# Cross-attention and feed-forward: values computed and placed early, three written orders, one sum per tile

## The chip, the cores and the metric

The kernel runs on one core of a Trainium2 chip. The metric is the device time of the kernel in microseconds (us), the median of several executions; one more execution was recorded by the profiler, and all rows below come from that one.

## What is computed

`x` is 4 x 2048 rows of 512 numbers; each of the four batches has a context of 77 rows. 16 heads of 32.

```python
x = x + xattn(layernorm(x), ctx, mask, Wq, Wk, Wv, Wo)
#   q = xn @ Wq.T; k = ctx @ Wk.T; v = ctx @ Wv.T           (per head 32 wide)
#   probs = softmax(mask(q @ k.T / sqrt(32)))               (77 keys)
#   xattn = (probs @ v) @ Wo.T
x = x + ffn(layernorm(x), Win, bin_, W1, b1, W2, b2, Wout, bout)
#   s = xn @ Win + bin_                                      (64 units)
#   h = relu(s[..., None] * W1 + b1)                         (16 inner values each)
#   g = sum(h * W2, -1) + b2;  ffn = g @ Wout + bout
```

## The kernel before

**Groups and steps.** The 8192 rows are cut into 16 groups of 512 rows, each of 4 tiles of 128 rows. Matrix products run in float16 with a high and a low part of each operand, in three passes, so most values exist as two halves, "high" written by ScalarE (ACT) and "low" by VectorE (DVE) or GpSimd (POOL). The program is a software pipeline of steps i = -2 to 17. Step i works on five groups at once: AHEAD is the layer norm of group i+2, FRONT the queries of group i+1 (`q`, four 128-wide pieces), SOFT the softmax of group i, its `pv` and `wo` for tiles 0 and 1, BACK the rest of group i-1 (`pv` and `wo` of tiles 2 and 3, then `ffn_in` and the units `pre` 0 to 3), FFN the rest of group i-2 (`pre` 4 to 7, `g`, `out`, and the store). The softmax goes by eight halves k of a group (a tile has two halves of 8 heads x 77 keys, 616 columns): logits on PE (`lg`), `maxima` on DVE (row maximum, subtract), `exps` on ACT, `sums` on DVE for a tile (row sums, scaling, reciprocal), `divide` on POOL, `p_part` on ACT, `p_low` on POOL, and a transposing transfer `turn_p`. Steps -2 to 1 are written out, steps 2 to 13 are three laps of a hardware loop of four steps, and steps 14 to 17 are written out.

**Order.** Nothing is scheduled by a tool: each engine has one function `one_step` that lists its work in order, and runs it in that order, waiting on semaphores. One `one_step` serves all 20 steps; work whose group does not exist in a step is left out. PSUM is handed out by two rings of two banks each (`tr_banks`, `mm_banks`) in the order of the tables `TR_ORDER` and `MM_ORDER`.

**Transfers.** All transfers are issued by SyncE's queue (SP), in order, and a transfer that must wait holds everything behind it: `turn_p`, `turn_x`, `turn_h` (transposes of the probabilities and of the two normed inputs), `store`, `reload` of x (two halves a group), `next_keys`, and `next_values`. The latter fills `v_now`, two buffers of blocks of V as `pv` wants them: 12 transfers (`CUTS`) from `v_all` for one buffer, at every even step from 2 to 12; step 0 fills both buffers, 24 transfers. In the queue they stand behind `turn_p(3)` and ahead of `turn_x(0)`, `turn_h(2)` and `turn_h(3)`.

**Setup.** Before step -2, PE transposes the context, Wk and Wq and makes the keys. Wv and Wo (the part LATE: `late_values`, `late_wo`) come in step 0, between `wo(2)` and `pv(0, .)` in the lists: 16 transposes of Wv, 32 matmuls for V of four batches, 16 transposes of Wo. Small weights of the feed-forward part lie in the second buffer of `qT`, so the first piece of q of group 1 in step 0 (`q_part` on ACT) waits until `wout` has been placed by 16 transfers.

Of the kernel before, what the change touches and what calls it, by code (L numbers as in the profile page):

```python
# [67 lines left out]
ALL = (AHEAD, FRONT, SOFT, BACK, FFN)  # L68
FIRST_FULL = 2
# [5 lines left out]
TR_ORDER = (  # L75
    (FFN, "pre", 4), (FFN, "pre", 5), (FFN, "pre", 6), (FFN, "pre", 7), (FRONT, "q", 0), (FRONT, "q", 1),
    (FRONT, "q", 2), (FRONT, "q", 3), (LATE, "wvT", 0), (LATE, "wvT", 1), (LATE, "wvT", 2), (LATE, "wvT", 3),
    (LATE, "woT", 0), (LATE, "woT", 1), (LATE, "woT", 2), (LATE, "woT", 3), (BACK, "pre", 0), (BACK, "pre", 1),
    (BACK, "pre", 2), (BACK, "pre", 3),
)  # L80
MM_SETUP = [("k", c) for c in range(C)]
MM_ORDER = (
    (FFN, "g", 0), (FFN, "out", 0), (FFN, "out", 1), (FFN, "out", 2), (FFN, "out", 3), (BACK, "pv", 2),
    (BACK, "pv", 3), (BACK, "wo", 2), (LATE, "v", 0), (LATE, "v", 1), (LATE, "v", 2), (LATE, "v", 3), (BACK, "wo", 3),
    (SOFT, "pv", 0), (SOFT, "pv", 1), (SOFT, "wo", 0), (SOFT, "wo", 1), (BACK, "s", 0),
)
# [62 lines left out]
class Ring:  # L149
# [3 lines left out]
    def __init__(self, setup, order, tensor, ready, free):  # L153
        self.setup, self.order, self.tensor, self.ready, self.free = setup, order, tensor, ready, free

    def uses(self, i):
        return sum(part in parts_of(i) for part, _, _ in self.order)

    def base(self, step):

        if step is SETUP:
            return 0
        if isinstance(step.i, int):
            return len(self.setup) + sum(self.uses(i) for i in range(-1, step.i))
        return len(self.setup) + sum(self.uses(i) for i in range(-1, FIRST_FULL))
# [7 lines left out]
    def place(self, step, name, k):  # L173
        if step is SETUP:
            return self.setup.index((name, k))
        return self.base(step) + [(n, m) for part, n, m in self.order if part in step.parts].index((name, k))
# [25 lines left out]
def build(nc, x, ctx_in, mask, Wq, Wk, Wv, Wo, Win, bin_, W1, b1, W2, b2, Wout, bout, out):  # L202
    stack = ExitStack()
    with stack:
# [19 lines left out]
        v_all = sb("v_all", [KEYS, B, 2, 2 * HC, 2 * DK], F16)  # L224
        v_now = sb("v_now", [P, 2, 2, len(CUTS), 2 * DK], F16)
        wv_raw = sb("wv_raw", [P, C, D], F32)
# [18 lines left out]
        h_normed = sb("h_normed", [P, 2, D], F32)  # L245
        x_parts = sb("x_parts", [P, 2, 2, D], F16)
        h_parts = sb("h_parts", [P, 2, 2, D], F16)
# [17 lines left out]
        row_sum = sb("row_sum", [P, 2, 2, 2 * HC], F32)  # L265
# [4 lines left out]
        w_raw = [pT_f[:, C * D * n:C * D * (n + 1)].rearrange("p (c n) -> p c n", c=C) for n in range(2)]  # L270
        w_raw += [wv_raw[:, :, :]]
# [6 lines left out]
        spare = qT[:, 1, :, :, :].rearrange("p a c r -> p (a c r)").bitcast(F32).rearrange("p (s n) -> p s n", s=4)  # L278
# [56 lines left out]
        v_ready = [sem("v_ready_0"), sem("v_ready_1")]  # L335
        a_high = sem("a_high")
# [35 lines left out]
        def _(sp):  # L372
# [67 lines left out]
            def turn_p(step, k):  # L440
# [5 lines left out]
                if k == 4 and g.n > 0:  # L446
                    mm.wait_ready(sp, home, "pv", 3)
# [951 lines left out]
```

## Time and profile before

| | |
|---|---|
| median of 3 runs | 976.37 us (975.87 to 976.71) |
| profiled execution, its own time | 980.87 us |
| its span | 979.1 us, granted TensorE clock 0.928 |
| PE busy | 799.1 us, 82% of the span |
| DVE, ACT, POOL busy | 660.0, 536.4, 529.1 us |
| steps -2 to 1 (start to the first logits of step 2) | 189.8 us |
| steps 2 to 13 (three laps) | 210.3, 212.2, 209.7 us |
| steps 14 to 17 | 157.1 us |

The profiled execution has a time of its own, 1.8 us above its span and 4.5 us above the median; sums over the trace are made against it. A busy share is an average over stages: in the first 189.8 us PE is busy for 125.6 us, in the loop for 558.8 us of 632.2.

### The profile page before, as it was taken

To read this page: it belongs to the slowest core of one execution; us is meant where nothing else is said; L and a number is where in the kernel's file an instruction comes from. 1 tells how busy PE (TensorE), PEld (TensorE's weight loads), DVE (VectorE), ACT (ScalarE), POOL (GpSimd) and SP (SyncE) were. 2 spreads that over 40 slices of the span, in tenths; PEclk is the share of its full clock that TensorE was granted. 3 is DMA by queue.
4 is the path that set the end of the run, shared out by engine and by line. 5 is a ranking of instruction groups with operands and counts; after the bars stand their busy time and mean duration, and the time that the engine had idled before them with its cause. 6 is when DMAs were issued, how large, how long until landed. Compare 5 with 4: busy or idle time off the path is not lost.

```text
span 979.1 us, 17043 instructions
## 1 busy us (share of the span) xinstructions
PE 799.1 (82%) x5778; PEld 382.9 (39%) x5778; DVE 660.0 (67%) x1199; ACT 536.4 (55%) x835; POOL 529.1 (54%) x499
## 2 busy tenths in 40 slices
PE   6257769897989799797989796988989798987745
PEld 5123334444444445252534343443535353533221
DVE  2145257876787778686878777676888687776632
ACT  2344245746666566657484757456665748363712
POOL 5124028664757565656575665556575657455520
PEclk9678979998999999899999999898999899998988
DMA  9513026483847567564858394655666585626231
GB/s 338 129 45 59 4 54 129 89 188 76 187 101 174 103 146 136 94 146 104 185 105 177 84 190 96 133 133 115 152 129 127 112 175 113 124 58 137 60 101 44
DMA packets 336084, 118.78 MB, mean 121 GB/s; under 512 B 324652, under 2 KB 325316, under 8 KB 335992
## 3 DMA queue, kind: packets, MB, share of 16 engines
q1 hardware_dynamic: 335415, 116.97, 54.7%
q8 instruction: 50, 0.82, 0.3%
q10 hardware_dynamic: 576, 0.64, 0.2%
q14 instruction: 43, 0.34, 0.1%
HBM read 22.64 MB, written 16.78 MB: 40 GB/s over the span
## 4 chain that ended last, share of the span: by engine, by line
PE 50%; DVE 10%; issue 10%; POOL 9%; SPq 8%; ACT 7%; DMA 5%; ACTq 0%; POOLq 0%; DVEq 0%
PE mm_banks L1189 12%; PE tr_banks L1189 10%; PE lg_banks L1226 5%; SPq L413 5%; PE mm_banks L1244 5%; PE mm_banks L1290 5%; POOL p_parts L609 4%; POOL probs L603 3%; PE mm_banks L1301 3%; ACT inner L781 2%; PE tr_banks L1281 2%; PE lg_banks L1223 2%; DVE probs L984 2%; DVE row_max L980 2%; PE mm_banks L1181 2%
## 5 line engine op out<-in xcount | busy, mean ns | idle before, releaser
L609 POOL TENSOR_TENSOR p_parts<-probs,p_parts 128x616 f16<-128x616 f32 x128 | 172.6, 1355 | 89.0 <-ACT p_parts L761 87.5
L1189 PE MATMUL tr_banks<-xT,wqT 128*128 128x512 f16 x768 | 179.2, 388 | 32.9 <-DMA xT<-x_parts 27.8
L603 POOL TENSOR_TENSOR probs<-probs,row_inv 128x616 f32<-128x616 f32 x128 | 154.3, 1216 | 66.9 <-DVE row_inv L1000 66.9
L1189 PE MATMUL mm_banks<-woT,aT 128*128 128x512 f16 x768 | 173.4, 383 | 10.4 <-DVE aT L1006 5.6
L1226 PE MATMUL lg_banks<-k_blocks,qT 128*128 128x308 f16 x768 | 151.0, 313 | 0.0
L753 ACT ACTIVATE probs<-probs 128x616 f32<-128x616 f32 x128 | 89.4, 710 | 72.3 <-DVE probs L984 71.7
L587 POOL TENSOR_TENSOR x_parts<-x_normed,x_parts 128x512 f16<-128x512 f32 x64 | 74.0, 1156 | 101.5 <-ACT x_parts L722 101.3
L1189 PEld LDWEIGHTS tr_banks<-xT,wqT 128*128 128x128 f16 x768 | 73.8, 99 | 135.3 <-issue 48.3
L984 DVE TENSOR_TENSOR probs<-lg_banks,row_max 128x616 f32<-128x616 f32 x128 | 102.4, 800 | 32.6 <-POOL p_parts L609 22.5
L761 ACT ACTIVATE p_parts<-probs 128x616 f16<-128x616 f32 x128 | 90.9, 710 | 49.7 <-POOL probs L603 45.6
L1189 PEld LDWEIGHTS mm_banks<-woT,aT 128*128 128x128 f16 x768 | 74.5, 98 | 103.8 <-issue 14.4
L980 DVE TENSOR_REDUCE row_max<-lg_banks 128x8 f32<-128x616 f32 x128 | 100.7, 787 | 16.8 <-PE lg_banks L1226 14.9
L781 ACT ACTIVATE inner<-tr_banks,inner_cols,w_div 128x512 f32<-128x512 f32 x128 | 94.3, 771 | 29.2 <-PE tr_banks L1281 28.9
L994 DVE TENSOR_REDUCE row_sum<-probs 128x8 f32<-128x616 f32 x128 | 98.2, 788 | 8.4 <-issue 4.8
L1281 PE MATMUL tr_banks<-s_parts,spread 128*128 128x512 f16 x128 | 49.0, 440 | 58.8 <-DVE s_parts L1039 42.4
L1226 PEld LDWEIGHTS lg_banks<-k_blocks,qT 128*128 128x128 f16 x768 | 79.5, 104 | 41.7 <-issue 3.5
L1223 PE MATMUL lg_banks<-mask_bias,ident 128*128 128x308 bf16 x256 | 81.8, 319 | 13.7 <-issue 7.6
L592 POOL TENSOR_TENSOR h_parts<-h_normed,h_parts 128x512 f16<-128x512 f32 x64 | 74.1, 1157 | 16.6 <-ACT h_parts L740 16.6
L1244 PE MATMUL mm_banks<-pT,v_now 128*32 128x256 f16 x2304 | 70.6, 278 | 12.5 <-DMA v_now<-v_all 9.4
L712 ACT ACTIVATE x_normed<-xr,shift,rstd 128x512 f32<-128x512 f32 x64 | 51.6, 806 | 50.9 <-POOL shift L572 49.5
L765 ACT ACTIVATE aT<-mm_banks 128x512 f16<-128x512 f32 x64 | 38.1, 597 | 74.2 <-PE mm_banks L1244 74.2
L578 POOL TENSOR_TENSOR rstd<-var_eps,neg_half 128x2 f32<-128x2 f32 x32 | 22.3, 696 | 102.9 <-DVE var_eps L1028 102.9
(93 smaller groups left out, 990.9 us busy)
## 6 DMA issues: line engine op xcount, KB each, us to landing
xr<-in_x SPq DMA_DIRECT2D x32, 512.0 KB, 5.7
out_x<-xr SPq DMA_DIRECT2D x32, 512.0 KB, 2.9
pT<-p_parts SPq DMA_TRANSPOSE x128, 3.6
k_blocks<-kT_all SPq DMA_DIRECT2D x32, 38.5 KB, 2.3
pT<-in_L_xattn_Wk SPq DMA_DIRECT2D x1, 1024.0 KB, 8.9
pT<-in_L_xattn_Wq SPq DMA_DIRECT2D x1, 1024.0 KB, 13.0
wv_raw<-in_L_xattn_Wv SPq DMA_DIRECT2D x1, 1024.0 KB, 15.2
hT<-in_L_xattn_Wo SPq DMA_DIRECT2D x1, 1024.0 KB, 16.5
```

The source lines that it names most:

```text
L603: pool.tensor_tensor(block_of(k), block_of(k), inv, ALU.mult).then_inc(probs_ready, 1)
L609: pool.tensor_tensor(p_parts[:, k % PS, 1, 0:2 * LW], probs[:, k % 4, :], p_parts[:, k % PS, 0, 0:2 * LW], ALU.subtract).then_inc(p_lowere ...
L753: act.activation(probs[:, k % 4, :], probs[:, k % 4, :], ACT.Exp, scale=DK ** -0.5 / W_SCALE)\
L761: act.activation(p_parts[:, k % PS, 0, 0:2 * LW], probs[:, k % 4, :], ACT.Copy).then_inc(p_high, 1)
L781: tr.read(act.activation(inner[:, j % IN_SLOTS, :], tr.bank(step, "pre", j), ACT.Relu, bias=inner_cols[:, 1, j:j + 1], scale=w1_div[:, j:j ...
L980: dve.tensor_reduce(top, logits, AX.X, ALU.max).then_inc(max_done, 1)
L984: dve.tensor_tensor(probs_of(k), logits, top.unsqueeze(3).broadcast_to([P, 2, HC, KEYS]), ALU.subtract)\
L994: dve.tensor_reduce(row_sum[:, 0, u, :], probs[:, k % 4, :].rearrange("p (h k) -> p h k", k=KEYS), AX.X, ALU.add).then_inc(sum_done, 1)
L1189: last = pe.matmul(bank, stationary(a, c), moving(b, c), start=(n == 0), stop=(n == len(passes) - 1))
L1223: pe.matmul(bank.rearrange("p (h k) -> p h k", k=KEYS), ident16[:, :], mask_bias[:, g.slot, t, :].unsqueeze(1).broadcast_to([P, HC, KEYS]) ...
L1226: last = pe.matmul(bank, qT[:, g.parity, qp, c, rows], k_blocks[:, buffer, kp, c, :], start=False, stop=(m == 2))
L1244: last = pe.matmul(bank[rows, cols], v_now[:, buffer, b, CUTS.index(cut), DK * vp:DK * (vp + 1)], pT[:, pair, b, pp, n, :], start=((vp, pp ...
```

## The change

It has four parts. (1) LATE moves from step 0 to step -2: Wv and Wo are transposed and V is made right behind the transposes of Wq. To make room, Wq has a buffer of its own, Wv is loaded into the second buffer of `qT`, the small weights move into `pT` (so `turn_p(4)` of group 0 waits for `wout`, and `q_part` no longer does), and V lies in the space of the normed inputs of the feed-forward part. (2) The 12 transfers that cut V into blocks are made once for batch 0 in step -2 and once for batches 1 to 3 in step 0 (`v_blocks`); a change of batch is then one transfer of 128 x 1536 float16 from `v_blocks` to `v_now`, at the end of an even step. (3) Every engine has three lists, `fill_step` for steps -2 to 0, `loop_step` for 1 to 13, `drain_step` for 14 to 17, and the rings have three orders. (4) `sums` takes the 1232 columns of a tile in one reduction, when both halves are there; its 16 results lie on every second element of `row_sum`, and the scaling and the reciprocal read them so.

```diff
 def parts_of(i):
-    return parts + (LATE,) if i == 0 else parts
+    return parts + (LATE,) if i == -2 else parts
...
-        def run(eng, one_step):
-            for i in range(-2, FIRST_FULL):
-                one_step(Step(0, i))
+        def run(eng, fill_step, loop_step, drain_step):
+            for i in range(-2, 1):
+                fill_step(Step(0, i))
+            for i in range(1, FIRST_FULL):
+                loop_step(Step(0, i))
             with eng.Fori(0, LOOPED // 4, 1) as t:
                 for v in range(FIRST_FULL, FIRST_FULL + 4):
-                    one_step(Step(t, v))
+                    loop_step(Step(t, v))
             for i in range(FIRST_FULL + LOOPED, GROUPS + 2):
-                one_step(Step(0, i))
+                drain_step(Step(0, i))
...
-            def values(buffer, batch):
-                for i, (n, h, key, first, size) in enumerate(CUTS):
-                    sp.dma_start(v_now[first:first + size, buffer, :, i, :], v_all[key:key + size, batch, :, h, :])\
-                        .then_inc(v_ready[buffer], 16)
...
+            def place_values(step):                       # SP, step -2, ahead of turn_x(0)
+                sp.wait_ge(pool_const, 15)
+                mm.wait_read(sp, step, "v", 0)
+                for i, (n, h, key, first, size) in enumerate(CUTS):
+                    sp.dma_start(v_now[first:first + size, 0, i, :], v_all[key:key + size, 0, h, :])\
+                        .then_inc(v_ready[0], 16)
+            def place_rest(step):                         # SP, step 0, behind turn_p(3)
...
+                sp.dma_start(v_now[:, 1, :, :].rearrange("p i n -> p (i n)"),
+                             v_now[:, 0, :, :].rearrange("p i n -> p (i n)")).then_inc(v_ready[1], 16)
...
+                for i, (n, h, key, first, size) in enumerate(CUTS):
+                    sp.dma_start(v_blocks[first:first + size, :, i, :], v_all[key:key + size, 1:B, h, :])\
+                        .then_inc(v_placed, 16)
+            def next_values(step):                        # SP, even steps, last in the step
+                buffer, batch = (0, (step.i + 2) // 4) if step.i % 4 == 2 else (1, step.i // 4)
+                if step.i % 2 == 0 and 0 < batch < B:
...
                     mm.wait_ready(sp, step, "pv", 3)
+                    sp.dma_start(v_now[:, buffer, :, :].rearrange("p i n -> p (i n)"),
+                                 v_blocks[:, batch - 1, :, :].rearrange("p i n -> p (i n)")).then_inc(v_ready[buffer], 16)
...
             def sums(step, tile):
-                for u in range(2):
-                    k = 2 * tile + u
-                    dve.wait_ge(exp_done, 2 * n + u + 1)
-                    dve.tensor_reduce(row_sum[:, 0, u, :], probs[:, k % 4, :].rearrange("p (h k) -> p h k", k=KEYS),
-                                      AX.X, ALU.add).then_inc(sum_done, 1)
-                dve.wait_ge(sum_done, 2 * n + 2)
-                dve.tensor_scalar(row_sum[:, 1, :, :], row_sum[:, 0, :, :], 1.0 / P_SCALE, None, ALU.mult)\
+                k = 2 * tile % 4
+                dve.wait_ge(exp_done, 2 * n + 2)
+                dve.tensor_reduce(row_sum[:, 0, :, :, 0].rearrange("p u h -> p (u h)"), probs[:, k:k + 2, :].rearrange(
+                    "p u (h k) -> p (u h) k", k=KEYS), AX.X, ALU.add).then_inc(sum_done, 1)
+                dve.wait_ge(sum_done, n + 1)
+                dve.tensor_scalar(row_sum[:, 1, :, :, 0], row_sum[:, 0, :, :, 0], 1.0 / P_SCALE, None, ALU.mult)\
                     .then_inc(scaled, 1)
                 dve.wait_ge(scaled, n + 1)
-                dve.reciprocal(row_inv[:, tile, :, :], row_sum[:, 1, :, :]).then_inc(inv_done, 1)
+                dve.reciprocal(row_inv[:, tile, :, :], row_sum[:, 1, :, :, 0]).then_inc(inv_done, 1)
```

PE's order in the fill, step 0 before: the last three pieces of q, then the transposes of Wv (`wv_raw`), the products for V, logits, the transposes of Wo (they lie in `hT`) and the first `pv`:

```order
L1189 MATMUL tr_banks<-xT,wqT 128x512 x36
L1161 MATMUL tr_banks<-ident,wv_raw 128x128 x16
L1181 MATMUL mm_banks<-aT,inner 77x512 x16
L1223 MATMUL lg_banks<-mask_bias,ident 128x308
L1226 MATMUL lg_banks<-k_blocks,qT 128x308 x3
L1223 MATMUL lg_banks<-mask_bias,ident 128x308
L1226 MATMUL lg_banks<-k_blocks,qT 128x308 x3
L1161 MATMUL tr_banks<-ident,hT 128x128 x16
L1244 MATMUL mm_banks<-pT,v_now 32x256 x72
```

The same stretch of work after, where it now stands, from the transposes of Wk (`pT`) and the products for the keys to the first piece of q of group 0; `wq_raw`, `qT` and `hT` are the raw Wq, Wv and Wo:

```order
L1553 MATMUL tr_banks<-ident,pT 128x128 x16
L1562 MATMUL mm_banks<-inner,aT 128x308 x16
L1553 MATMUL tr_banks<-ident,wq_raw 128x128 x16
L1553 MATMUL tr_banks<-ident,qT 128x128 x16
L1573 MATMUL mm_banks<-aT,inner 77x512 x16
L1553 MATMUL tr_banks<-ident,hT 128x128 x16
L1581 MATMUL tr_banks<-xT,wqT 128x512 x48
```

The transposes of Wv and Wo and the 32-instruction product for V moved from behind the queries of step 0 to the gap ahead of the first query, and nothing of them is left between the logits and the first `pv`.

SP's queue in an even step of the loop before, from the middle of the 12 transfers of `next_values` to the end of the transposes of x and h:

```order
L413 DMA v_now<-v_all 76x2x64
L413 DMA v_now<-v_all 1x2x64
L413 DMA v_now<-v_all 77x2x64
L413 DMA v_now<-v_all 50x2x64
L413 DMA v_now<-v_all 27x2x64
L413 DMA v_now<-v_all 77x2x64
L429 DMA_TRANSPOSE xT<-x_parts 128x8x128
L437 DMA_TRANSPOSE hT<-h_parts 128x8x128 x2
L429 DMA_TRANSPOSE xT<-x_parts 128x8x128 x3
L437 DMA_TRANSPOSE hT<-h_parts 128x8x128 x2
```

And after, from `turn_p(2)` and `turn_p(3)` to the end of an even step; L410 is `reload(1)` of x:

```order
L480 DMA_TRANSPOSE pT<-p_parts 128x10x128 x2
L410 DMA xr<-in_x 128x1024
L465 DMA_TRANSPOSE hT<-h_space 128x8x128 x2
L457 DMA_TRANSPOSE xT<-x_parts 128x8x128 x3
L465 DMA_TRANSPOSE hT<-h_space 128x8x128
L457 DMA_TRANSPOSE xT<-x_parts 128x8x128
L465 DMA_TRANSPOSE hT<-h_space 128x8x128
L530 DMA v_now<-v_blocks 128x1536
```

The 12 transfers are gone from ahead of the transposes; one transfer stands behind them. The second half of the load of x, which stood ahead of `turn_p(1)`, is now behind `turn_p(3)`, and both `hT` transposes of tiles 2 and 3 stand ahead of the transposes of x.

PE's order at the end of a step of the loop before: `wo(0)` and `wo(1)`, the logits of half 6, `ffn_in` and the first two units:

```order
L1189 MATMUL mm_banks<-woT,aT 128x512 x24
L1215 REGISTER_ALU
L1223 MATMUL lg_banks<-mask_bias,ident 128x308
L1226 MATMUL lg_banks<-k_blocks,qT 128x308 x3
L1223 MATMUL lg_banks<-mask_bias,ident 128x308
L1226 MATMUL lg_banks<-k_blocks,qT 128x308 x3
L1262 REGISTER_ALU
L186 REGISTER_ALU
L1273 MATMUL mm_banks<-hT,win 64x512 x12
L195 REGISTER_ALU
L186 REGISTER_ALU
L1281 MATMUL tr_banks<-s_parts,spread 128x512 x2
```

After, from the same `wo(0)` and `wo(1)`; the logits are now those of half 7:

```order
L1581 MATMUL mm_banks<-woT,aT 128x512 x24
L1654 REGISTER_ALU
L213 REGISTER_ALU
L1665 MATMUL mm_banks<-hT,win 64x512 x12
L1607 REGISTER_ALU
L1615 MATMUL lg_banks<-mask_bias,ident 128x308
L1618 MATMUL lg_banks<-k_blocks,qT 128x308 x3
L1615 MATMUL lg_banks<-mask_bias,ident 128x308
L1618 MATMUL lg_banks<-k_blocks,qT 128x308 x3
L222 REGISTER_ALU
L213 REGISTER_ALU
L1673 MATMUL tr_banks<-s_parts,spread 128x512 x2
```

`ffn_in` now follows the products of `wo` directly, and the last logits of the group stand between it and the units, which before stood right behind it.

On ACT, a step of the loop has after `s_part` (which releases `pre` 0): `x_part(2)`, `x_part(3)`, `h_normal(0)`, `h_normal(1)`, `h_part(0)` and only then `relus(0)`; before, `relus(0)` followed one exponential and the two `h_normal`. On DVE, `x_statistics(1)` (the second half of x) stands ahead of `a_low(0, .)`, without which `wo(0)` does not begin, as before.

## Rows read from the trace of the kernel before

**Rows 1.** Stretches: the loop, then step 3; columns stand in the first line.

```profile
core 0: us, PE busy (x) PEld busy (x) DVE busy (x) ACT busy (x) POOL busy (x), PEclk, DMA share, GB/s
189.80:822.00 632.20, 558.77 (x4225) 266.57 (x4225) 484.01 (x877) 387.10 (x600) 387.43 (x361) 0.95 0.63 134
243.40:293.70 50.30, 45.61 (x353) 21.96 (x352) 41.33 (x75) 32.46 (x51) 32.59 (x32) 0.99 0.65 140
```

**Rows 2.** Timeline of SP, step 4: start, duration, line, transfers.

```profile
322.94 10.27 SPq L413 DMA_DIRECT2D v_now<-v_all  x12
```

**Rows 3.** Timeline of PE, end of step 4; in brackets the idle time before.

```profile
339.02 1.49 PE L1273 MATMUL mm_banks<-hT,win 128*64 128x512 f16 x12 [2.88 <-DMA hT<-h_parts]
343.14 0.60 PE L1281 MATMUL tr_banks<-s_parts,spread 128*128 128x512 f16 x2 [2.64 <-DVE s_parts L1039]
```

**Rows 4.** Timeline of PE, end of step 7, which changes no values.

```profile
501.37 1.03 PE L1281 MATMUL tr_banks<-s_parts,spread 128*128 128x512 f16 x2 [2.88 <-DVE s_parts L1039]
```

**Rows 5.** Timeline of PE at the end of the loop's first lap.

```profile
400.15 0.43 PE L1223 MATMUL lg_banks<-mask_bias,ident 128*128 128x308 bf16 x1 [3.64 <-issue]
```

**Rows 6.** Timeline of PE in steps -2 to 1.

```profile
14.78 10.92 PE L1170 MATMUL mm_banks<-inner,aT 128*128 128x308 f32 x32 [0.78 <-ACT aT L671]
27.55 1.25 PE L1161 MATMUL tr_banks<-ident,pT 128*128 128x128 f32 x8 [0.98 <-DVE wqT L910]
46.10 12.60 PE L1189 MATMUL tr_banks<-xT,wqT 128*128 128x512 f16 x48 [17.30 <-DMA xT<-x_parts]
...
71.88 5.28 PE L1189 MATMUL tr_banks<-xT,wqT 128*128 128x512 f16 x12 [10.46 <-DMA xT<-x_parts]
...
98.33 15.52 PE L1181 MATMUL mm_banks<-aT,inner 128*77 128x512 f32 x32 [0.89 <-ACT aT L683]
...
127.42 4.03 PE L1244 MATMUL mm_banks<-pT,v_now 128*32 128x256 f16 x72 [9.41 <-DMA v_now<-v_all]
...
148.01 3.41 PE L1189 MATMUL tr_banks<-xT,wqT 128*128 128x512 f16 x12
```

**Rows 7.** Timeline of ACT in steps -2 to 0.

```profile
29.34 0.80 ACT L712 ACTIVATE x_normed<-xr,shift,rstd 128x512 f32<-128x512 f32 x1
...
82.28 0.60 ACT L747 ACTIVATE qT<-tr_banks 128x512 f16<-128x512 f32 x1 [6.61 <-DMA wout<-qT]
...
113.89 0.59 ACT L687 ACTIVATE v_all<-mm_banks 77x512 f16<-77x512 f32 x1 [2.84 <-PE mm_banks L1181]
```

**Rows 8.** Timeline of SP in steps -1 and 0.

```profile
70.24 10.79 SPq L527 DMA_DIRECT2D wout<-qT  x16
84.94 11.21 SPq L449 DMA_TRANSPOSE pT<-p_parts  x4
115.31 20.77 SPq L413 DMA_DIRECT2D v_now<-v_all  x24
```

**Rows 9.** Timeline of PE in step 15.

```profile
895.24 7.80 PE L1189 MATMUL mm_banks<-woT,aT 128*128 128x512 f16 x24 [4.17 <-DVE aT L1006]
...
907.66 5.34 PE L1189 MATMUL mm_banks<-woT,aT 128*128 128x512 f16 x24 [0.31 <-issue]
```

**Rows 10.** Groups of DVE instructions by line and shape: busy us, mean ns.

```profile
L994 DVE TENSOR_REDUCE row_sum<-probs 128x8 f32<-128x616 f32 x128 | 98.2, 788 | 8.4 <-issue 4.8 <-ACT probs L753 0.8
L997 DVE TENSOR_SCALAR row_sum<-row_sum 128x16 f32<-128x16 f32 x64 | 30.6, 478 | 2.2
```

**Rows 11.** Timeline of DVE, a scaling whose source is strided.

```profile
92.80 1.08 DVE L963 TENSOR_SCALAR minus_mean<-mean_var 128x4 f32<-128x4 f32 x1
93.79 0.16 DVE L964 TENSOR_SCALAR var_eps<-mean_var 128x4 f32<-128x4 f32 x1
```

**Rows 12.** Timeline of POOL, the same time.

```profile
91.19 2.66 POOL L609 TENSOR_TENSOR p_parts<-probs,p_parts 128x616 f16<-128x616 f32 x2
```

**Rows 13.** Timeline of ACT at the end of step 4.

```profile
340.31 0.63 ACT L722 ACTIVATE x_parts<-x_normed 128x512 f16<-128x512 f32 x1 [2.82 <-DMA xT<-x_parts]
```

**Rows 14.** Page, transfers: the load of x, us from issue to landing.

```profile
xr<-in_x SPq DMA_DIRECT2D x32, 512.0 KB, 5.7
```

More of the change, by code:

```diff
@@ L68 @@
 ALL = (AHEAD, FRONT, SOFT, BACK, FFN)
+FILL, LOOP, DRAIN = "fill", "loop", "drain"
 FIRST_FULL = 2
@@ new lines, in place_wout, with fill_step @@
+            def place_wout(step):
+                if step.i != 0:
+                    return
+                sp.wait_ge(wout_high, 1)
+                sp.wait_ge(wout_low, 1)
+                for j in range(J):
+                    for part in range(2):
+                        sp.dma_start(wout[unit_rows(j, part), :], wout_parts[MJ * j:MJ * (j + 1), part, :])\
+                            .then_inc(wout_placed, 16)
+            def fill_step(step):
+                ahead, soft, late = (AHEAD in step.parts, SOFT in step.parts, LATE in step.parts)
+                if late:
+                    place_values(step)
+                if soft:
+                    place_wout(step)
+                    turn_p(step, 0)
+                    turn_p(step, 1)
+                    next_values(step)
+                    turn_p(step, 2)
+                    turn_p(step, 3)
+                    place_rest(step)
+                if ahead:
+                    turn_x(step, 0)
+                    turn_x(step, 1)
+                    turn_x(step, 2)
+                if soft:
+                    turn_h(step, 0)
+                if ahead:
+                    turn_x(step, 3)
+                if soft:
+                    turn_h(step, 1)
@@ new lines, in loop_step @@
+                if back:
+                    h_normal(step, 2)
+                    h_part(step, 2)
+                if soft:
+                    a_part(step, 0, 1)
+                if back:
+                    h_normal(step, 3)
+                    h_part(step, 3)
+                if ahead:
+                    x_normal(step, 0)
+                    x_part(step, 0)
+                    x_normal(step, 1)
+                    x_part(step, 1)
+                    x_normal(step, 2)
+                if front:
+                    q_part(step, 3)
@@ new lines, in loop_step @@
+                if ahead:
+                    x_normal(step, 3)
+                if soft:
+                    exps(step, 6)
+                if back:
+                    s_part(step)
+                if ahead:
+                    x_part(step, 2)
+                    x_part(step, 3)
+                if soft:
+                    h_normal(step, 0)
+                    h_normal(step, 1)
+                    h_part(step, 0)
+                if back:
+                    relus(step, 0)
+                if soft:
+                    exps(step, 7)
@@ L1071, in one_step @@
                     sums(step, 0)
+                if ffn:
+                    output(step, 0)
+                    output(step, 1)
+                if soft:
+                    maxima(step, 2)
+                if ffn:
+                    output(step, 2)
+                if soft:
+                    maxima(step, 3)
+                if ffn:
+                    output(step, 3)
+                if soft:
+                    sums(step, 1)
+                if back:
+                    a_low(step, 1, 0)
+                    a_low(step, 1, 1)
@@ L1335, in one_step @@
                 if soft:
+                    logits(step, 2)
                     logits(step, 3)
```

773 lines of the change are left out of this document (571 added, 202 removed).

## Prediction, made before the changed kernel ran

> **What bounds the kernel now.** I read the page first (busy shares and the chain), then the stretches of the span, then the timelines of PE, SP and ACT where PE stands still. PE is busy for 82% of the span, but unevenly. In the loop (steps 2 to 13) it works 558.8 of 632.2 us [rows 1], so the loop is bound by PE, its waits and its clock. In steps -2 to 1 it works 125.6 of 189.8 us, and there chains of other engines and SP's queue set the time.
>
> In the loop, a step that changes no values takes 50.3 us with PE busy for 45.6 [rows 1]. Half of the steps change values. SP then issues 12 transfers for 10.27 us [rows 2]; the transposes of h stand behind them, and PE stops for 2.88 us ahead of `ffn_in` for the late `hT` [rows 3]. In a plain step `ffn_in` finds its operand, and the only large wait is the one behind it, 2.88 us until DVE has `s_parts` [rows 4]. After it PE runs at its lower level for a while: the pair of unit matmuls takes 1.03 us there and 0.60 in step 4 [rows 3, 4]. At each end of a lap 3.64 us go to the loop itself [rows 5].
>
> In the fill, PE waits 17.30 us for the first x, 10.46 before the first q of step 0 (ahead of it DVE and ACT make the small weights), then works 15.52 on V, and waits 9.41 for the 24 transfers of values [rows 6]. The first norm of group 0 starts at 29.34 on ACT [rows 7], the first q at 46.10.
>
> **Part A, values early: -25 us.** The V products now fall into PE's 17.3 us wait. The transposes of Wq end at 28.8 [rows 6]; eight transposes with their wait took 2.23 us, so 16 take about 4.5; V's 32 instructions begin at about 33.3 and take at most the 15.5 that they took before, less if PE, which no longer pauses ahead of them, starts at its full clock. They end by 47.5 to 48.8. In the list of ACT the copies of V stand ahead of the norm of group 0, so ACT does not reach `x_normal(0)` until then: 18 to 20 us later than 29.34. The 12 transfers of `place_values` (0.87 us each, by 20.77 for 24 [rows 8]: 10.4 us) stand ahead of `turn_x(0)`, but can start behind the first copy of V and are done when the norm is. Before, 16.8 us lay between the norm and q, behind the loads of the weights; I take 12 to 13 for the same chain with its queue empty, an estimate, so q starts near 60, 14 us late. Of these some 5 come back, because the norm of group 1 is now listed ahead of the last two pieces of q: step 0 starts 9 us late.
>
> Step 0 then loses more than that. Before, the four transposes of p were issued by 96.15, and `pv` began at 127.42 because V was not made and placed [rows 6, 8]. After, SP is the chain: the 16 transfers of `wout` end at 81.0 + 9 = 90; four transposes of p take 6 to 11.2 us (11.2 before, with waits); `place_rest` issues 13 transfers, 11.3 us; from there to the q of step 1 it was 11.9 us (136.08 to 148.01). That gives 119.2 to 124.4 against 148.01, a gain of 23.6 to 28.8; I take 25, at the lower side because ACT's 6.61 us wait for `wout` [rows 7] moves to SP and does not vanish whole. Bounds: 16, if group 0's norm is late by a further 9 us (V at PE's lower level: the key products took 341 ns for 308 columns [rows 6], 567 for 512, 18.1 us in all; and the 16.8 us chain in place of 12.5), and 33, if the 9 us are hidden. POOL's additional memset, of `v_blocks`, costs nothing: it stands behind that of `v_now`, and its first reader is `place_rest`, near 96 us.
>
> **Part B, the loop: -18 us.** 12 x 50.3 = 603.6 and two ends of a lap 7.3 make 610.9; the loop takes 632.2, so 21.3 us are what the six value steps cost above a plain step, 3.5 each. One transfer behind the last transpose takes SP a single issue, and the waits for `hT` go. I keep 0.5 us for each of the six, since its 393 KB travel beside the first transposes of p of the next step (a 512 KB load takes 5.7 us to land [rows 14]): -18. Bounds: 0 to -21.
>
> The new order of a plain step I cost at nothing. What it moves is `lg` 7 into the 2.88 us wait, which would give about 1 us of PE a step; but `ffn_in` now follows `wo(1)` directly, where `lg` 6 covered the last norm's transposes, and between the units only ACT's relu is left to wait for. Gain and loss lie within 1.5 us a step, 18 us, either way; this is the widest term, and the rivals below have it.
>
> **Part C, the drain: -7 us.** In step 15 `wo(2)` waits 4.17 us for `aT` and then runs for 7.80 us where it takes 5.34 at full clock [rows 9]. In the drain list logits stand there and `out(0)` too, which takes both: 6.6 us. The chain at the end, from the last `pv` to the last store, has nothing in it that the change removes. Bounds 0 to -15.
>
> **Part D, the sums: 0.** One reduction of 616 columns takes 0.788 us, a 16-column instruction 0.16 when nothing disturbs it [rows 10, 11]. A reduction of 1232 columns is then about 2 x 0.788 - 0.15 = 1.43 us, 9 us less of DVE's work in 64 tiles. DVE does not end the steps of the loop, so PE's time covers it. Where DVE does wait for the second exponential (step 0 and the drain) the answer comes 0.64 us later than with two reductions; with some four such places 2 to 3 us, which I leave within the bounds of A and C.
>
> The scaling took 478 ns in the mean, 0.3 us above 0.16 [rows 10], because it can wait for POOL: line 963, whose source is already strided, took 1.08 us, and ended at 93.88, when POOL's two instructions of 91.19 ended (93.85) [rows 11, 12]. So a stride alone did not free that instruction there, and I let the new scaling wait as before. The Trainium skill says the same in "Vector Engine (DVE) Microarchitecture Reference", section 5.1 Performance modes: the mode in which a one-source instruction takes both ports, and so excludes GpSimd, asks for SBUF operands and an even outer size, not for adjacent elements; by it the stride is no remedy and the sum stands; were it one, the sum would be some 5 us lower (the last rival). Row 963 is on its side.
>
> **Sum.** 980.87 - 25 - 18 - 7 = 930.9 for the profiled execution; its own time was 4.5 us above the median, so 926.4: I predict 926.
>
> **Rivals.**
> *The load of x comes just too late* (0.25). `reload(1)` now stands behind `turn_p(3)`, where the 12 transfers began: 29.2 us into step 4 (322.94 - 293.7). Issued there and landing 5.7 us later it is there at 34.9 to 35.7; two statistics and two `a_low`, at most 0.79 each, follow on DVE, so `wo(0)` can start at 37.7 to 38.9. PE would be ready for it about 12 us ahead of the step's end (two products of `wo` 5.3, `ffn_in` 1.5, the wait 2.9 [rows 3, 4, 9]; units and relus 2.4, an estimate from 0.30 a unit and as much again for waits), at 38.2. The margin is nothing. At 1.5 us a step, PE's pause and its lower clock after it together, 12 steps lose 18 us: 944.
>
> *Slower than before* (0.10). On ACT `relus(0)` now stands behind `x_part(3)`, two `h_normal` and `h_part(0)`. In step 4 `x_part(3)` waited 2.82 us for a transpose of x [rows 13], and SP issues those behind both transposes of h, which wait for POOL. Each unit from the third waits for a relu to free its bank, so a late `relus(0)` holds PE to the end of the step. If `relus(0)` comes 1 us late, 12 us are lost, as above. The change ends slower when the loop loses more than A and C give: (25 + 7 + 18) / 12 = 4.2 us in each step. Against it: without the 10.27 us of transfers the transposes of x are issued earlier in half of the steps, and ACT is busy for only 32.5 of 50.3 us. At 5 us a step: 926 + 60 = 986; for the lower part of this case the result is about the same as before.
>
> *PE stays at its upper level* (0.10). If work fills the 2.88 us wait well enough that the units and logits behind it keep their 0.60 us, a step loses about 1.3 us of half-clock work: 12 x 1.3 = 16, and 910.
>
> *The strided scaling is free of POOL* (0.05). The change would then take 0.3 us from the sums of each tile, of which those in the fill and the drain, some 16, stand on a chain: 5 us, 921.
>
> The forecast itself has 0.50. **Range.** 900 is about the third rival with Part A at its 33; 956 the first with Part A and C 12 us short. A change of 0.2% (2 us) is about what a measurement of this kernel can tell from none. All cases but the second are faster by more than that; of its 0.10 I give 0.07 to slower and 0.03 to the same.
>
> **What would show it.** A: V's products near 33 us, the first q near 60, `pv` of step 0 near 103, the first logits of step 2 near 165. B: one transfer in place of 12 and no 2.88 us ahead of `ffn_in`; even and odd steps alike, near 50.3; if `wo(0)` waits for `aT` behind a load of x, the first rival holds, if the third unit waits for relus, the second. C: no 4 us ahead of `wo(2)` in step 15. D: a reduction of 1.43 us, and scalings of which some still take over 1 us. The forecast is wrong if plain steps leave 50.3 by more than 1.5 us either way, or if the first logits of step 2 are not between 157 and 174.

## The result, and the profile after

The changed kernel takes 940.28 us (median of 4, 938.53 to 940.77) against 976.54 before: a ratio of 0.9626, 95% interval 0.9609 to 0.9643. It is faster, as forecast, and 14 us above the forecast of 926. The profiled execution took 940.77 us, its span 939.0. From the page of after, the span, PE's busy time and the chain by engine; the last line is the same chain of before:

```profile
span 939.0 us, 16872 instructions
PE 798.3 (85%) x5778; PEld 377.6 (40%) x5778; DVE 663.6 (71%) x1135; ACT 535.2 (57%) x835; POOL 530.9 (57%) x500
PE 72%; DVE 10%; ACT 5%; issue 5%; POOL 3%; DMA 3%; SPq 0%; ACTq 0%; POOLq 0%; DVEq 0%
```

```profile
PE 50%; DVE 10%; issue 10%; POOL 9%; SPq 8%; ACT 7%; DMA 5%; ACTq 0%; POOLq 0%; DVEq 0%
```

SP has left the chain, PE has taken its place. The stretches of after: steps -2 to 1, the loop, step 8 within it (it changes values), step 14, steps 15 to 17 (columns as in [rows 1]):

```profile
0.00:163.60 163.60, 118.59 (x723) 63.85 (x724) 91.69 (x169) 79.07 (x129) 79.64 (x82) 0.89 0.49 126
163.60:785.40 621.80, 556.62 (x4225) 263.34 (x4226) 487.69 (x829) 385.78 (x601) 386.08 (x360) 0.93 0.65 138
474.70:525.80 51.10, 46.32 (x353) 21.96 (x353) 40.74 (x70) 32.14 (x52) 32.20 (x30) 0.93 0.65 138
785.40:832.80 47.40, 45.04 (x354) 21.63 (x354) 36.54 (x60) 26.98 (x43) 27.61 (x25) 0.96 0.52 96
832.80:939.00 106.20, 78.06 (x481) 28.75 (x479) 47.72 (x80) 43.33 (x65) 37.60 (x35) 0.73 0.40 92
```

| stretch | before | after | change | forecast |
|---|---|---|---|---|
| A, steps -2 to 1 | 189.8 | 163.6 | -26.2 | -25 |
| B, loop | 632.2 | 621.8 | -10.4 | -18 |
| C, steps 14 to 17 | 157.1 | 153.6 | -3.5 | -7 |
| profiled execution | 980.87 | 940.77 | -40.1 | -50 |

The rest of the 14 us is the profiled execution of before, which stood 4.5 us above its median; that of after stands 0.5 above.

**The fill.** PE in steps -2 to 1 (the rows that answer to [rows 6]), then the last copy of the values on ACT and the norm behind it:

```profile
31.72 13.93 PE L1573 MATMUL mm_banks<-aT,inner 128*77 128x512 f32 x32 [0.89 <-ACT aT L856]
...
55.06 1.97 PE L1553 MATMUL tr_banks<-ident,hT 128*128 128x128 f32 x8 [8.54 <-DVE woT L1213]
58.11 12.39 PE L1581 MATMUL tr_banks<-xT,wqT 128*128 128x512 f16 x48 [1.08 <-DVE woT L1213]
...
100.69 2.15 PE L1636 MATMUL mm_banks<-pT,v_now 128*32 128x256 f16 x72 [0.74 <-DMA pT<-p_parts]
...
122.19 5.00 PE L1581 MATMUL tr_banks<-xT,wqT 128*128 128x512 f16 x12 [6.39 <-DMA xT<-x_parts]
```

```profile
45.68 0.59 ACT L860 ACTIVATE h_space<-mm_banks 77x512 f16<-77x512 f32 x1 [2.84 <-PE mm_banks L1573]
46.18 0.80 ACT L886 ACTIVATE x_normed<-xr,shift,rstd 128x512 f32<-128x512 f32 x1
```

V is made while PE waited before; the norm follows the last copy at once, 16.8 us later than before. ACT's copies of Wo stand behind the norm in turn, and PE waits 8.54 us for them before its second half of Wo and the first q. That q is at 58.1 instead of 46.1, the first `pv` at 100.7 instead of 127.4, the q of step 1 at 122.2 instead of 148.0.

**The loop.** PE at the end of step 8, a value step, and ACT beside it:

```profile
517.33 1.49 PE L1665 MATMUL mm_banks<-hT,win 128*64 128x512 f16 x12
...
522.32 0.68 PE L1673 MATMUL tr_banks<-s_parts,spread 128*128 128x512 f16 x2 [2.34 <-DVE s_parts L1331]
523.87 0.61 PE L1673 MATMUL tr_banks<-s_parts,spread 128*128 128x512 f16 x1 [0.87 <-ACT inner L955]
525.40 0.61 PE L1673 MATMUL tr_banks<-s_parts,spread 128*128 128x512 f16 x1 [0.92 <-ACT inner L955]
```

```profile
522.54 0.61 ACT L917 ACTIVATE h_space<-h_space 128x512 f16<-128x512 f32 x1
523.06 0.76 ACT L955 ACTIVATE inner<-tr_banks,inner_cols,w_div 128x512 f32<-128x512 f32 x1
523.96 0.72 ACT L927 ACTIVATE probs<-probs 128x616 f32<-128x616 f32 x1
524.59 0.76 ACT L955 ACTIVATE inner<-tr_banks,inner_cols,w_div 128x512 f32<-128x512 f32 x1
```

The wait for `hT` ahead of `ffn_in` is gone [rows 3], also in value steps. But the two waits of 0.87 and 0.92 us behind it are for ACT: its first relu stands behind `h_part(0)`, and the last exponential stands between the first and the second. Even and odd steps are now alike, at 51.1 and 50.9 us in the mean (a lap's end left out); before, the even ones took 53.7 and the odd ones 50.5, step 3 with its 50.3 [rows 1] among the shortest.

PE's longest waits in the loop by what ended them (us in total, times, longest), before and after:

```profile
PE tr_banks L1281 <- DVE s_parts L1039: 32.0, 12, 2.9
PE mm_banks L1273 <- DMA hT<-h_parts: 17.1, 6, 2.9
PE tr_banks L1281 <- ACT inner L781: 11.0, 17, 0.8
PE lg_banks L1223 <- issue: 7.6, 2, 4.0
```

```profile
PE tr_banks L1673 <- ACT inner L955: 28.5, 36, 1.1
PE tr_banks L1673 <- DVE s_parts L1331: 28.2, 12, 2.4
PE lg_banks L1615 <- issue: 8.5, 2, 4.3
```

The 17.1 us for `hT` are gone, and the units wait 17.5 us more for relus (`inner`).

### The profile page after: what moved, and what is told of

Read it like the earlier page. It is cut to its first block, busy times and chain, and to the rows that moved or that the text cites. A ratio compares the mean times of both kernels' runs of the same rounds, so it can differ in the third digit from the quotient of the medians.

```text
span 939.0 us, 16872 instructions
## 1 busy us (share of the span) xinstructions
PE 798.3 (85%) x5778; PEld 377.6 (40%) x5778; DVE 663.6 (71%) x1135; ACT 535.2 (57%) x835; POOL 530.9 (57%) x500
## 4 chain that ended last, share of the span: by engine, by line
PE 72%; DVE 10%; ACT 5%; issue 5%; POOL 3%; DMA 3%; SPq 0%; ACTq 0%; POOLq 0%; DVEq 0%
PE tr_banks L1581 17%; PE mm_banks L1581 17%; PE lg_banks L1618 9%; PE mm_banks L1636 7%; PE mm_banks L1682 5%; PE mm_banks L1693 4%; PE lg_banks L1615 3%; PE tr_banks L1673 3%; ACT inner L955 3%; PE mm_banks L1691 2%; DVE qT L1262 2%; PE mm_banks L1573 1%; POOL p_parts L719 1%; POOL probs L713 1%; DVE stats L1309 1%
## 5 line engine op out<-in xcount | busy, mean ns | idle before, releaser
L1581 PE MATMUL mm_banks<-woT,aT 128*128 128x512 f16 x768 | 171.0, 379 | 1.4 <-DVE aT L1298 0.6
L1273 DVE TENSOR_REDUCE row_max<-lg_banks 128x8 f32<-128x616 f32 x128 | 100.8, 787 | 46.8 <-PE lg_banks L1618 46.4
L1673 PE MATMUL tr_banks<-s_parts,spread 128*128 128x512 f16 x128 | 60.8, 496 | 66.7 <-DVE s_parts L1331 33.6
L1286 DVE TENSOR_REDUCE row_sum<-probs 128x16 f32<-128x1232 f32 x64 | 91.7, 1433 | 30.4 <-ACT probs L927 25.7
L702 POOL TENSOR_TENSOR h_space<-h_space 128x512 f16<-128x512 f32 x64 | 74.0, 1158 | 52.1 <-ACT h_space L917 52.1
L1636 PEld LDWEIGHTS mm_banks<-pT,v_now 128*32 128x32 f16 x2304 | 60.1, 99 | 24.2 <-issue 22.2
```

The lines of the kernel that those rows point to most:

```text
L1273: dve.tensor_reduce(top, logits, AX.X, ALU.max).then_inc(max_done, 1)
L1286: dve.tensor_reduce(row_sum[:, 0, :, :, 0].rearrange("p u h -> p (u h)"), probs[:, k:k + 2, :].rearrange("p u (h k) -> p (u h) k", k=KEYS) ...
L1581: last = pe.matmul(bank, stationary(a, c), moving(b, c), start=(n == 0), stop=(n == len(passes) - 1))
L1636: last = pe.matmul(bank[rows, cols], v_now[:, buffer, CUTS.index(cut), DK * (2 * b + vp):DK * (2 * b + vp + 1)], pT[:, pair, b, pp, n, :], ...
```

## The experiments

All twelve ran beside the kernel before. Times are medians of six executions; the stretches are from each run's one profiled execution (first logits of step 2, loop, the rest).

| run | us | ratio, 95% interval | step 2 at | loop | rest |
|---|---|---|---|---|---|
| changed kernel again | 941.97 | 0.9659 (0.9630 to 0.9688) | 164.4 | 624.4 | 152.2 |
| dense sums | 941.02 | 0.9654 (0.9625 to 0.9683) | 163.1 | 624.7 | 149.7 |
| two sums | 943.11 | 0.9665 (0.9637 to 0.9694) | 165.0 | 625.0 | 152.1 |
| relus ahead | 924.73 | 0.9487 (0.9459 to 0.9515) | 162.5 | 606.1 | 150.0 |
| one transfer, old place | 941.36 | 0.9652 (0.9623 to 0.9680) | 163.0 | 624.1 | 152.2 |
| 12 transfers, new place | 939.32 | 0.9642 (0.9610 to 0.9674) | 163.5 | 626.3 | 147.8 |
| 12 transfers, old place | 941.55 | 0.9650 (0.9622 to 0.9679) | 163.9 | 624.4 | 150.1 |
| loop lists in the drain | 952.84 | 0.9753 (0.9722 to 0.9785) | 164.3 | 624.3 | 162.8 |
| before, one transfer | 966.34 | 0.9904 (0.9871 to 0.9936) | 194.7 | 614.2 | 156.8 |
| relus ahead, 12 transfers | 925.50 | 0.9481 (0.9455 to 0.9506) | 162.6 | 607.9 | 153.1 |
| relus ahead, norm first | 926.56 | 0.9463 (0.9426 to 0.9501) | 161.3 | 610.3 | 153.6 |
| the same, statistics first | 919.01 | 0.9430 (0.9406 to 0.9455) | 155.8 | 610.0 | 153.6 |

**The changed kernel again**, without an edit. 

> The changed kernel once more, beside the three below: 940 us (938 to 941).


941.97 us (940.72 to 944.06): 1 us above the expected range; it is the reference for the runs below.

**The sums.** Two runs take part (4) of the change apart. Dense:

```diff
-                dve.tensor_scalar(row_sum[:, 1, :, :, 0], row_sum[:, 0, :, :, 0], 1.0 / P_SCALE, None, ALU.mult)\
+                dve.tensor_scalar(row_sum[:, 1, :, :], row_sum[:, 0, :, :], 1.0 / P_SCALE, None, ALU.mult)\
...
```

> The changed kernel with its row sums side by side instead of on every second element, all else as it is. Theory (a stride does not free the scaling from POOL): the scaling, line 1289, keeps a mean of about 0.61 us with some over 1 us, and the time stays within 2 us of the changed kernel's. Rival (the stride helps): the mean of the scaling rises by 0.2 us or more and the time by up to 5 us.

Two sums, the old ones:

```diff
-                dve.wait_ge(exp_done, 2 * n + 2)
-                dve.tensor_reduce(row_sum[:, 0, :, :, 0].rearrange("p u h -> p (u h)"), probs[:, k:k + 2, :].rearrange(
+                for u in range(2):
+                    dve.wait_ge(exp_done, 2 * n + u + 1)
+                    dve.tensor_reduce(row_sum[:, 0, u, :], probs[:, k % 4, :].rearrange("p (h k) -> p h k", k=KEYS),
...
```

> The changed kernel with the old sums: two reductions of 616 columns for a tile, results side by side. Theory (DVE has cover): DVE's busy time rises by about 9 us, less whatever the scaling waits differently, and the time stays within 2 us. First rival (the one reduction comes 0.64 us late where DVE waits for the second exponential): 2 to 4 us faster than the changed kernel. Second rival (DVE's work counts): up to 9 us slower.

Both are within 1.2 us of the changed kernel's 941.97, with ranges that overlap, so in each the theory of unchanged time holds. The groups of DVE's sums, first of after, then the scaling of dense, then of two sums:

```profile
L1286 DVE TENSOR_REDUCE row_sum<-probs 128x16 f32<-128x1232 f32 x64 | 91.7, 1433 | 30.4 <-ACT probs L927 25.7 <-issue 4.7
L1289 DVE TENSOR_SCALAR row_sum<-row_sum 128x16 f32<-128x16 f32 x64 | 39.3, 614 | 2.2
```

```profile
L1289 DVE TENSOR_SCALAR row_sum<-row_sum 128x16 f32<-128x16 f32 x64 | 39.2, 613 | 2.2
```

```profile
L1290 DVE TENSOR_SCALAR row_sum<-row_sum 128x16 f32<-128x16 f32 x64 | 38.5, 601 | 2.2
```

614 ns with a stride, 613 without: the stride does nothing. The scaling takes longer than before (478 ns, [rows 10]) in all three, with the old sums too, so it comes from the new lists; that they put it beside POOL's work more often is likely, but was not counted.

**Relus ahead.** The diff is in ACT's `loop_step`:

```diff
                     h_normal(step, 1)
+                if back:
+                    relus(step, 0)
+                    relus(step, 1)
+                if soft:
                     h_part(step, 0)
-                if back:
-                    relus(step, 0)
-                if soft:
                     exps(step, 7)
-                if back:
-                    relus(step, 1)
-                if soft:
                     h_part(step, 1)
```

> The changed kernel with ACT's first two relus of a loop step moved ahead of the first low part of h and of the last exponential. Theory: a plain step takes 51.1 us after and 50.3 before because PE's third and fourth unit wait 0.9 us each for relus that stand behind other work on ACT; the third unit should start 0.4 us and the fourth 1.3 us earlier, so a step takes 50.0 to 50.4 and the kernel 928 to 932 us. Rival (the waits are the relu's own time in the two banks, or the last exponential, now later, holds the next step): 51 us a step and 938 to 942 us.

924.73 us, 17 below the changed kernel, and the loop 606.1: the theory held, and somewhat more was gained than it said. (This profile is the fastest of its six executions, 4.4 us under the median; the run with relus ahead and 12 transfers, profiled at its median, has 607.9 for the loop.) A step takes 49.3 to 50.3 us without a lap's end. PE at the end of step 8 in this run:

```profile
512.69 0.94 PE L1671 MATMUL tr_banks<-s_parts,spread 128*128 128x512 f16 x2 [2.34 <-DVE s_parts L1329]
514.07 1.27 PE L1671 MATMUL tr_banks<-s_parts,spread 128*128 128x512 f16 x2 [0.45 <-ACT inner L955]
```

The third unit starts 1.38 us after the first, not 1.55, and the fourth follows it without a wait; the units end 2.65 us after the first begins (515.34), not 3.69 (526.01): 1.0 us a step. Most of that is the second relu, which the exponential had held. PE's granted clock in the loop rose from 0.93 to 0.95 with it. Over the whole loop the waits for relus fell from 28.5 us to 15.3, and the wait behind `ffn_in` stayed:

```profile
PE tr_banks L1671 <- DVE s_parts L1329: 28.2, 12, 2.4
PE tr_banks L1671 <- ACT inner L955: 15.3, 29, 0.7
```

**Where did the 18 us of the transfers go?** Three runs vary number and place in the new lists. One transfer at the old place: the call of `next_values` in `loop_step` stands behind `reload(step, 1)`. Twelve:

```diff
-                    sp.dma_start(v_now[:, buffer, :, :].rearrange("p i n -> p (i n)"),
-                                 v_blocks[:, batch - 1, :, :].rearrange("p i n -> p (i n)")).then_inc(v_ready[buffer], 16)
+                    for i in range(len(CUTS)):
+                        sp.dma_start(v_now[:, buffer, i, :], v_blocks[:, batch - 1, i, :]).then_inc(v_ready[buffer], 16)
...
```

> The changed kernel with its one transfer for a change of batch moved ahead of the transposes of h and x (behind the load of x's second half). Theory (the number of transfers is what cost, not their place): SP has a pause there now, one issue of 0.6 us fits in, and the time stays within 2 us of the changed kernel's 941. Rival (the place ahead of the transposes is what cost): 2.9 us of wait ahead of the feed-forward product in six steps, 955 or more.

> The changed kernel with a change of batch as 12 transfers again, at the new place behind the last transpose of an even step. Theory (SP has no 10 us to spare on that path): the first transposes of p of the next step are issued 9.7 us later, the product of p and v of tiles 2 and 3 waits, and six steps lose 3 to 4 us each: 958 to 966. Rival (only the place mattered): within 3 us of 941.

> The changed kernel with a change of batch as 12 transfers at the old place, ahead of the transposes of h and x. Theory: the second part of the change is worth here what it was costed at, 3 us in each of six steps: 957 to 962, with a wait of 2 to 3 us ahead of the feed-forward product in even steps. Rival (the new lists leave SP a pause there that takes the 12 transfers): 941 to 946.

All three are at 939 to 942: neither the number nor the place costs anything that can be told from the spread in the new lists. The first theory held; the other two, which put a price of 16 us or more on the 12 transfers, fell. SP in step 8 of the run with 12 transfers at the old place, then PE there:

```profile
504.67 8.35 SPq L531 DMA_DIRECT2D v_now<-v_blocks  x12
513.07 2.67 SPq L465 DMA_TRANSPOSE hT<-h_space  x2
```

```profile
517.85 1.49 PE L1666 MATMUL mm_banks<-hT,win 128*64 128x512 f16 x12
```

SP works 8.35 us on them, and the transposes of h are behind them, yet PE does not wait: in after SP pauses there, since the next transposes wait for POOL's half of h until 511.25:

```profile
503.05 0.69 SPq L410 DMA_DIRECT2D xr<-in_x  x1
511.25 3.59 SPq L465 DMA_TRANSPOSE hT<-h_space  x2
```

The transfers put them off by less than 2 us, and the h transposes, which now go ahead of x's, are still in time. Which move in the lists made this pause was not taken apart. Nor was it traced why 12 transfers at the new place cost nothing.

The other side of the question is the old lists, with one transfer at the old place. `change` is one transfer from `v_blocks` to a buffer of `v_now`, `place_rest` the 12 transfers into `v_blocks`:

```diff
...
-                    values(1, step.i // 4)
+                    change(1, step.i // 4)
...
+                if step.first(0):
+                    place_rest()
...
```

> The kernel before, with its lists, and a change of batch as one transfer at the old place; the blocks of one batch are placed once, by 12 transfers at the end of step 0, and serve all later batches (so batches 2 and 3 use the values of batch 1). Theory (in the old lists the number of transfers was what six steps lost 3.5 us by): the loop falls from 632 to 612 to 616 us, and step 1 grows by up to 10 us for the extra placing. Rival (the number does not matter there either, since with the new lists 12 transfers cost nothing): the loop stays at 629 us or more.

```profile
194.70:808.90 614.20, 555.58 (x4225) 265.23 (x4224) 483.72 (x877) 386.87 (x601) 387.01 (x361) 0.97 0.65 140
```

And PE at the end of step 4 there, without the 2.88 us of [rows 3]:

```profile
337.68 1.49 PE L1291 MATMUL mm_banks<-hT,win 128*64 128x512 f16 x12
```

The loop falls from 632.2 to 614.2 us: 18.0, the number forecast, and all of it in the steps that change values (50.7 us in the mean, 53.7 before). The profiled span falls by 13.3, since placing the blocks moves step 2 back by 4.9 us. The median falls by 9, from 975.51 beside it, which the profiled execution of before exceeded by 5.4; by the medians the loop would have gained some 14 us, so that 18.0 was met to the tenth is in part luck. Its loop is 7.6 us shorter than that of the changed kernel: alone, the one transfer does about what it was costed at; in the new lists the wait that it removes is not there.

Whether this holds once the relus no longer hold PE:

> The kernel with the relus moved ahead (925 us), and a change of batch as 12 transfers at the old place ahead of the transposes. Theory (SP's pause ahead of the transposes of h takes them): within 3 us of 925. Rival (the pause covered them only as long as PE lost time to the relus): 2 us or more in each of six steps, 937 or more.

925.50 against 924.73. It holds.

**The drain.** `drain_step` replaced by `loop_step` in all five lists, and the order of banks with it:

> The changed kernel with the loop's lists, and the loop's order of PSUM banks, in steps 14 to 17 too. Theory (the drain lists gain 3 us in step 14 and in step 15 and lose as much behind the last transposes of h, where the last products run at PE's lower level): the last 153.6 us become 155 to 159 with the end behind the last transposes of h back at 23 to 24 us from 28: 943 to 947. Rival (the drain lists are worth the 7 us forecast): 948 or more. Second rival (they are a loss): below 939.

952.84: 11 us slower than the changed kernel, all of it behind the loop (162.8 us). The first rival held: against the new loop lists the drain lists are worth more than forecast. Against the old list they gave 3.5 us in the profile, and why not 7 stands below.

**The norm first.** A test of Part A's delay: in step -2, ACT does the norm of group 0 between the copies of the values, and SP's `place_values` moves behind the four transposes of x.

```diff
                 if late:
-                    late_values(step)
-                if ahead:
+                    x_normal(step, 0)
+                    wv_copy(step, 0)
+                    x_part(step, 0)
+                    wv_copy(step, 1)
...
```

> The kernel with the relus moved ahead (925 us), and in step -2 the norm of group 0 on ACT between the copies of the values, its transposes on SP ahead of the placing of values. Theory (the first q is late by what stands ahead of the norm on ACT, and the delay runs on to step 2): the first q starts at 48 to 51 us instead of 57 to 58, the first logits of step 2 at 153 to 157 instead of 162.5, the kernel takes 915 to 919. Rival (SP's chain of wout, p, the rest of the values and x sets steps 0 and 1, whenever q starts): first q earlier, the first logits of step 2 after 160, 922 to 926.

The first q came at 59.6, the kernel at 926.56: the theory fell. The times are close to the rival's (step 2 at 161.3), but q was not earlier, as the rival has it. The reason is one that I had not thought of:

```profile
34.77 0.81 ACT L886 ACTIVATE x_normed<-xr,shift,rstd 128x512 f32<-128x512 f32 x1 [5.21 <-POOL shift L682]
```

In the changed kernel DVE's statistics of group 0 stand behind the low parts of the keys and of Wq, so in this run the norm could not start before 34.8, and what I had listed behind it, the copies of Wv, waited too. The last run moves the statistics ahead of these on DVE, and the first copy of Wv ahead of the norm on ACT:

> As the kernel with the relus moved ahead and the norm of group 0 between the copies of the values, and on DVE the statistics of group 0 ahead of the keys' and queries' low parts, where the kernel before has them (the run with the norm first had its norm wait for them until 34.8 us, and the copies of the values with it); the first copy of Wv stands ahead of the norm. Theory (the norm, once it is not behind the values, no longer sets the first q; PE's V work does): the norm starts near 29 us, V near 33 to 35, the first q at 51 to 54 us instead of 57 to 58, the first logits of step 2 at 156 to 159 instead of 162.5, and the kernel takes 918 to 921. Rival (SP's chain sets steps 0 and 1): the first logits of step 2 after 160, 923 to 927.

```profile
54.03 10.52 PE L1598 MATMUL tr_banks<-xT,wqT 128*128 128x512 f16 x48 [0.91 <-DVE woT L1226]
```

The first q is at 54.0 (57.0 with the relus ahead alone), the first logits of step 2 at 155.8 (162.5), and the kernel takes 919.01 us (914.85 to 921.11), ratio 0.9430 (0.9406 to 0.9455): the best of all here, 21 us below the changed kernel. This theory held.

## Why the prediction was right, and where it was not

The direction was right, and 940 lies within the range of 900 to 956, 14 us above the 926. It lies nearest to the first rival's 944, but that rival's mechanism did not hold; the number alone would have misled.

**Part A held in size (26.2 for 25), and in its first half in mechanism.** V began at 31.7 (33.3), in PE's pause, the first q was at 58.1 (60), `pv` of step 0 at 100.7 (103) and no longer waited for values, step 2 at 163.6 (165). The last run shows that the delay of q had its price further on: q 3 us earlier there, step 2 6.7 us earlier. The chain told for step 0 is not the one in the trace. "SP is the chain" held for the length: from the end of `wout` at 89.7 us (90) to the q of step 1 it took 32.5 us (29.2 to 34.4). But in it SP stood 9.6 us for POOL (SP's waits from 78 to 123 us):

```profile
SPq L480 <- POOL p_parts L719: 5.1, 2, 4.0
SPq L465 <- POOL h_space L702: 2.4, 1, 2.4
SPq L457 <- POOL x_parts L697: 2.1, 1, 2.1
```

The forecast took such waits from the trace of before without naming what ends them; that the sum came out is in part luck. The 11.9 us between norm and q (12 to 13) also hold PE's 8.54 us for the copies of Wo, which the forecast has not.

**Part B failed in the term "the new order of a plain step I cost at nothing".** Its value half was right in size for the old lists: 18.0 us in the profiles, some 14 by the medians, shown by the run with them. But in the new lists the transfers cost nothing in any number or place tried, so the loop's gain comes from the lists, which remove the wait for `hT` by themselves; and the same lists bring new waits. By the steps, the six that change values are 15.2 us shorter in all, the four plain ones 1.8 longer, the two at a lap's end 3.0 longer: -10.4. By PE's waits, the 17.1 us for `hT` went, and those for relus rose by 17.5; the wait behind `ffn_in`, which the order was to fill, fell only from 32.0 to 28.2. (The term of 21.3 us, what the value steps cost above plain ones, was somewhat large too: six times 53.7 less 50.5 is 19.) That it is the place of the relus that costs is shown by the run that moves them: their waits fell to 15.3 us and the loop to 606.1. A plain step by itself is only 0.4 us longer than before, within the 1.5 that the term allowed; its size against a single step of before also hangs on the clock (PE busy 46.32 us at a granted 0.93 in step 8, 45.61 at 0.99 in step 3 of before).

**The rivals.** In step 8 DVE waited 0.27 us for the load of x, and was done 0.9 us before `wo(0)` at 512.06, which did not wait (the timeline of DVE); no product of `wo` in the loop waited:

```profile
506.94 1.29 DVE L1244 BATCH_NORM_STATS2 stats<-xr 128x6 f32<-128x512 f32 x2 [0.27 <-DMA xr<-in_x]
...
510.50 0.69 DVE L1298 SCALAR_TENSOR_TENSOR aT<-mm_banks,aT 128x512 f16<-128x512 f32 x1 [0.91 <-ACT aT L939]
```

The margin that I put at nothing was there: the load was issued 28.4 us into the step (29.2) and the statistics that read it began 3.9 us later (5.7). The second rival, `relus(0)` late on ACT, was the true mechanism, at 1.5 us of added waits a step and not at the 4.2 from which it would have decided; and most of what moving the relus gave back was an instruction that I had not named, the exponential between the first two. PE did not stay at its upper level at a step's end (third rival): the logits behind the units run at 0.97 us there.

**Part C** named step 15's wait for `aT`, and it went (4.17 to none; 0.63 for the second pair; the rows that answer to [rows 9]):

```profile
853.06 5.34 PE L1581 MATMUL mm_banks<-woT,aT 128*128 128x512 f16 x24
...
863.32 5.34 PE L1581 MATMUL mm_banks<-woT,aT 128*128 128x512 f16 x24 [0.63 <-DVE aT L1298]
```

But the last 106.2 us are as long as before (106.3), since PE ran at its lower level: granted 0.73 there, 0.90 before. With the same drain lists the other runs took 100.8 to 104.8 us for the same stretch, at a granted 0.78 to 0.86, and the shorter the higher it was (104.4 at 0.80, 101.4 at 0.85, 100.8 at 0.86). Step 14, 47.4 us here for 50.8 before, took 46.9 to 49.0 in them. So C is 3.5 to 9 us by the table's last column, and this profile fell at its low end; before has one profile alone. The same stretch, steps 15 to 17, in before and in the run with 12 transfers at the new place:

```profile
872.80:979.10 106.30, 68.30 (x481) 27.25 (x479) 50.58 (x87) 44.12 (x67) 40.41 (x37) 0.90 0.38 87
```

```profile
836.80:937.60 100.80, 69.17 (x481) 28.16 (x479) 47.62 (x80) 42.66 (x65) 37.59 (x35) 0.86 0.42 97
```

**Part D held**: the reduction takes 1.433 us (1.43), DVE is not faster for it in sum, since the scalings take 9 us more, and neither piece of it moves the time. The stride changed nothing, 614 ns with it and 613 without. The Trainium skill ("Vector Engine (DVE) Microarchitecture Reference", section 5.1 Performance modes) names no stride among the conditions of the mode in which a one-source instruction uses both read ports; the traces agree.

## What to carry to other kernels

Price a removed wait in the order of work in which it will stand, not in that where it was seen: some 18 us in the old lists were none in the new ones. Where two PSUM banks pass between PE and another engine, keep other work from between that engine's reads: here 1.3 us of it ahead of and between two relus cost PE 1 us in each of 12 steps. And when work is moved into a pause, read what the first instruction behind it waits for on every engine; the pause of 17 us had the norm, its statistics and the copies of Wo behind it.

## What was not expected of the hardware

PE's clock in the last 106 us differed between executions of one drain list by nearly as much as the whole of Part C: 106.2 us at 0.73, 100.8 at 0.86. In after it fell near 875 and, but for a spell near 900, stayed at the lower level to the end through pauses of at most 1.6 us, a wait of 2.47 us for p and one of 9.35 us for h; before, it stayed up through a pause of 2.72 us. Why is open.

The larger memset on POOL held a DVE instruction in the setup: the mask took 3.18 us, 0.80 before, and ended 0.66 after the memset. The timelines of DVE and POOL:

```profile
14.25 3.18 DVE L1189 TENSOR_SCALAR mask_bias<-probs 128x1232 bf16<-128x1232 int32 x1 [13.04 <-DMA probs<-in_mask_1x1xSxS_ik]
```

```profile
12.84 3.93 POOL L674 MEMSET v_blocks<- 128x4608 f16 x1
```

In the run of before with one transfer a shorter memset ended at 15.48 us, and the mask took 1.70 us and ended at 16.14, again 0.66 behind it; in every trace with the larger memset the mask took 2.9 to 3.3 us. So a POOL instruction that reads nothing held this DVE instruction, as those of [rows 12] held theirs. It cost nothing here: the logits that read the mask begin at 70 us.
